# In bucketing, GpSimd adds the products with the counts in pairs of tiles, in place of VectorE

## What is computed

```python
edge_index = jnp.stack([src, dst])
h = jnp.maximum(_layernorm(x, axis=-1), 0.0)
x = x + _L0_gnn_ref(h, L0_gnn_qW, L0_gnn_kW, L0_gnn_vW, src, dst)   # attention over edges, 4 heads
h = jnp.maximum(_layernorm(x, axis=-1), 0.0)
x = x + _L1_gnn_ref(h, src, dst, L1_gnn_W, L1_gnn_b)                # softmax aggregation, linear
h = jnp.maximum(_layernorm(x, axis=-1), 0.0)
x = x + _L2_gnn_ref(h, edge_index)                                  # 10 steps of propagation
h = jnp.maximum(_layernorm(x, axis=-1), 0.0)
x = x + _L3_gnn_ref(h, edge_index, L3_gnn_W1, L3_gnn_b1, L3_gnn_W2, L3_gnn_b2)
```

## Time and profile before

| | us |
|---|---|
| device time, median of 3 runs | 3986.82 (3985.64 to 3989.67) |
| profiled execution, device time | 3985.65 |
| its span | 3983.4 |
| TensorE matmuls busy | 3849.9 (97%) |
| VectorE busy | 1767.2 (44%) |
| ScalarE busy | 1296.6 (33%) |
| GpSimd busy | 598.4 (15%) |

### The profile page before, as it was taken

How to read it: one execution, slowest core, us unless ns; L and a number is a source line. 1 busy time by engine, 2 the same in 40 slices (tenths; PEclk the granted TensorE clock), 3 DMA queues, 4 the chain that set the end, 5 groups by cost and what they waited for, 6 DMA issues and landing times.

```text
span 3983.4 us, 124087 instructions
## 1 busy us (share of the span) xinstructions
PE 3849.9 (97%) x46183; PEld 3657.0 (92%) x46183; DVE 1767.2 (44%) x4392; ACT 1296.6 (33%) x3880; POOL 598.4 (15%) x716
## 2 busy tenths in 40 slices
PE   2889999999999999999999999999999998999999
PEld 2679999999966667999999999999999998999999
DVE  8999999999982333222222222222222222331111
ACT  1248888888850111222222122122222221111110
POOL 1016666666630000000000000000000000000000
PEclk9989999999999999999999999999999999999999
DMA  1039999999973333666656665665666655667675
GB/s 41 3 74 240 232 239 231 232 236 233 232 209 111 112 109 131 204 204 204 201 205 202 201 205 200 203 205 200 204 203 201 205 201 178 203 218 213 208 216 157
DMA packets 438000, 747.71 MB, mean 188 GB/s; under 512 B 197331, under 2 KB 330579, under 8 KB 437840
## 3 DMA queue, kind: packets, MB, share of 16 engines
q1 hardware_dynamic: 433346, 744.61, 61.6%
q10 hardware_dynamic: 4494, 0.77, 0.1%
HBM read 621.82 MB, written 83.32 MB: 177 GB/s over the span
## 4 chain that ended last, share of the span: by engine, by line
PE 92%; DVE 6%; issue 1%; ACT 0%; DMA 0%; ACTq 0%; POOL 0%; DVEq 0%; SPq 0%; POOLq 0%
PE sum L1843 49%; PE sum L1477 19%; PE pk L1195 10%; PE pr L1218 7%; PE pq L1207 3%; PE pc L1231 2%; DVE onerank L814 2%; PE l L490 1%; DVE bt L786 1%; DVE prodb L803 1%; DVE vals L796 1%; PE l L474 0%; DMA X<-in_x_dram 0%; PE sum L1668 0%; DVE kv L622 0%
## 5 line engine op out<-in xcount | busy, mean ns | idle before, releaser
L1843 PE MATMUL sum<-u,ring 128*128 128x192 f16 x12005 | 993.0, 246 | 0.0
L1843 PEld LDWEIGHTS sum<-u,ring 128*128 128x128 fp8e4 x12005 | 992.0, 98 | 0.3
L1843 PE MATMUL sum<-y,ring 128*128 128x192 f16 x11662 | 962.9, 246 | 0.0
L1843 PEld LDWEIGHTS sum<-y,ring 128*128 128x128 fp8e4 x11662 | 962.2, 98 | 0.0
L1477 PE MATMUL sum<-u,ring 128*128 128x385 f16 (+1 forms) x4802 | 607.2, 288 | 6.6 <-issue 5.2
L1477 PEld LDWEIGHTS sum<-u,ring 128*128 128x128 fp8e4 x4802 | 435.1, 98 | 168.0 <-issue 8.7
L1852 DVE TENSOR_TENSOR z<-lo,sum 128x96 f32<-128x96 f32 x441 | 112.1, 254 | 986.9 <-ACT lo L1867 986.7
L1195 PE MATMUL pk<-kv,hT 128*128 128x192 f16 x4900 | 485.7, 247 | 2.0 <-DVE hT L1087 2.0
L1195 PEld LDWEIGHTS pk<-kv,hT 128*128 128x128 f16 x4900 | 409.8, 99 | 2.4 <-DVE hT L1087 2.3
L1277 ACT ACTIVATE kvs<-pk 128x384 f32<-128x384 f32 x735 | 301.0, 437 | 111.4 <-PE pk L1195 90.9
L1218 PE MATMUL pr<-wv,hs_wide 128*128 128x101 f32 x2450 | 321.3, 278 | 2.0 <-POOL wv L1148 2.0
(11 more groups left out here) (252 smaller groups left out, 3033.8 us busy)
## 6 DMA issues: line engine op xcount, KB each, us to landing
ring<-adjacency_t SPq DMA_DIRECT2D x490, 800.0 KB, 4.3
ring<-adjacency SPq DMA_DIRECT2D x147, 896.0 KB, 5.0
rows<-slot_rows_d SPq DMA_DIRECT2D x249, 320.0 KB, 4.0
adjacency<-row SPq DMA_DIRECT2D x49, 800.0 KB, 4.3
adjacency_t<-col SPq DMA_DIRECT2D x49, 800.0 KB, 4.6
col<-row SPq DMA_TRANSPOSE x245, 4.2
out_dram<-X SPq DMA_DIRECT2D x6, 336.0 KB
slot_rows_d<-T SPq DMA_DIRECT2D x2, 240.0 KB
```

What stands on the lines that cost most here:

```text
L1843: m = pe.matmul(ps[r][:, 0:2 * D], w[:, t // 2, :, t % 2], n["this"][:, t, 0:2 * D], start=t == 0, stop=t == TILES - 1)
```

## The change

The addition `prod2` leaves VectorE's queue. GpSimd gets a loop over the 25 groups: wait for the group's `prod`, wait until TensorE has read the last group's `prod2` (`ranked`), add. It signals a new semaphore `halved`, for which TensorE waits at the head of `tensor_rank` beside `prod`. `k.prod` now counts one signal per group, and all waits on it are renumbered. A semaphore that was not used (`added2`) gives way to the new one.

```diff
--- before.py
+++ after.py
@@ -782,7 +782,7 @@
             if g >= 2:
                 v.wait_ge(k.counted.sem, k.counted.at(g - 1))
                 v.wait_ge(k.val.sem, k.val.at(g - 1))
-                v.wait_ge(k.prod.sem, k.prod.at(2 * (g - 1)))
+                v.wait_ge(k.prod.sem, k.prod.at(g - 1))
             v.tensor_tensor(bt[i][:], number_2[:].unsqueeze(1).to_broadcast([P, TWOS_RUN, TILES, 2]), of_group(tile1, g),
                             ALU.is_equal).then_inc(k.bt.sem, 1)
             if g >= 2:
@@ -798,12 +798,10 @@
         def vector_before(g):
             v.wait_ge(k.before.sem, k.before.at(g + 1))
             if g:
-                v.wait_ge(k.prod.sem, k.prod.at(2 * g))
+                v.wait_ge(k.prod.sem, k.prod.at(g))
                 v.wait_ge(k.ranked.sem, k.ranked.at(g))
             v.tensor_tensor(prod[:], bt[g % 2][:], before[g % 2][:].unsqueeze(1).to_broadcast([P, TWOS_RUN, TILES, 2]),
                             ALU.mult).then_inc(k.prod.sem, 1)
-            v.wait_ge(k.prod.sem, k.prod.at(2 * g + 1))
-            v.tensor_tensor(prod2[:], prod[:, :, 0:EVEN // 2, :], prod[:, :, EVEN // 2:EVEN, :], ALU.add).then_inc(k.prod.sem, 1)
 
         def vector_place(g):
             v.wait_ge(k.rank.sem, k.rank.at(g + 1))
@@ -819,6 +817,12 @@
             pool.iota(base[:], [[GROUP, GROUPS]], base=0, channel_multiplier=0,
                       allow_small_or_imprecise_dtypes=True).then_inc(k.base1.sem, 1)
             pool.memset(tile0, 0.0).then_inc(k.base1.sem, 1)
+            for g in range(GROUPS):
+                pool.wait_ge(k.prod.sem, k.prod.at(g + 1))
+                if g:
+                    pool.wait_ge(k.ranked.sem, k.ranked.at(g))
+                pool.tensor_tensor(prod2[:], prod[:, :, 0:EVEN // 2, :], prod[:, :, EVEN // 2:EVEN, :],
+                                   ALU.add).then_inc(k.halved.sem, 1)
 
         def tensor():
             for turn in range(GROUPS + 1):
@@ -876,7 +880,8 @@
             parts += [(far[i][:, odd, j, :], pr[:, TWOS_RUN:RUN]) for odd in range(2) for j in range(half)]
             parts += [(prod[:, :, j, :], to) for j in range(EVEN, TILES)] + [(prod2[:, :, j, :], to) for j in range(EVEN // 2)]
             pe.wait_ge(k.same.sem, k.same.at(2 * g + 2))
-            pe.wait_ge(k.prod.sem, k.prod.at(2 * g + 2))
+            pe.wait_ge(k.prod.sem, k.prod.at(g + 1))
+            pe.wait_ge(k.halved.sem, k.halved.at(g + 1))
             if g:
                 pe.wait_ge(k.rank.sem, k.rank.at(g))
             for n, (part, place_of) in enumerate(parts):
@@ -905,7 +910,7 @@
                 if turn < GROUPS:
                     a.wait_ge(k.counted.sem, k.counted.at(turn + 1))
                     if turn >= 2:
-                        a.wait_ge(k.prod.sem, k.prod.at(2 * (turn - 2) + 1))
+                        a.wait_ge(k.prod.sem, k.prod.at(turn - 1))
                     a.activation(before[turn % 2][:], over(pp[turn % 2][:, 0:TILES], 2), ACT.Copy).then_inc(k.before.sem, 1)
                     projection.copy(turn)
                 if turn == EARLY:
@@ -960,7 +965,8 @@
     k.weighted, k.summed = Beat(k, "at_weighted", CP), Beat(k, "at_summed", CP)
     k.q_in, k.denom, k.inverse, k.normed = (Beat(k, f"at_{x}", 2) for x in ("q_in", "denom", "inverse", "normed"))
     k.ratio, k.totalled, k.degreed = (Beat(k, f"at_{x}", 2) for x in ("ratio", "totalled", "degreed"))
-    k.added, k.added2 = k.sig("added"), k.sig("added2")
+    k.added = k.sig("added")
+    k.halved = k.sig("halved")
     k.row_out, k.col_out = ([Beat(k, f"at_{x}{b}", n) for b in range(2)] for x, n in (("row_out", 16 * CHUNKS + 16), ("col_out", 16)))
     k.out_c = Beat(k, "at_out_c", 2 * UP)
     k.av_set = k.sig("av_set")
```

## The result

The changed kernel takes 4027.05 us (median of 4, 4025.85 to 4030.66) beside 3986.69 us for the kernel before: a ratio of 1.0100, 95% interval 1.0088 to 1.0112. The direction was forecast; the time, 4069, was not, and the range missed it by one microsecond at its low end.

The account below looks back on a forecast made before the run. VectorE was taken to bound bucketing, with delays passed on in full; 24 turns each 3.38 us longer (81.1) plus 1.4 for the last gave 82.5 us, so 4069 us, range 4028 to 4088.

Parts of the forecast that it names:

- What bounds the stage; a delay passes on in full: Bucketing: VectorE sets the pace, busy 197.52 of 200.00 us; any shift of its end shifts the rest of the kernel.
- Removal: 0.65 us a turn: VectorE in bucketing: without prod2, bt starts 0.98 us after prodb in place of 1.63.
- Length of the addition, 2.0 us: GpSimd's addition over 128x864 16-bit elements, scaled from its fp32 rows; bounds 1.66 to 2.19 us.
- the low end of 1.0 us: GpSimd's addition, should 16-bit inputs go twice as fast: about 1.0 us, giving 4045 us.
- When GpSimd may begin: behind vals: Bucketing turn: VectorE's run bt, near, far, vals keeps GpSimd out; it starts 3.78 us after prodb's start.
- rows 7 and 8: Attention trace rows: GpSimd's weighting starts 0.09 us behind VectorE's hd, read as VectorE's run keeping GpSimd out.
- B: Rival in bucketing: GpSimd gets in right behind bt, adding from 2.14 to 4.14 us; 4030 us, chance 0.10.
- B's price, 1.74 us a turn: Bucketing turn under rival B: onerank at 6.73 us after prodb's start in place of 4.99; chance 0.10.
- Rank path as what is late: Bucketing: onerank waits for rankb, 2.55 us behind the addition, with VectorE idle for nearly 4 us.
- The clock, at most 3 us: TensorE idling more at 1.2 GHz lengthens the rank path by 0.12 us a turn, at most 3 us in all.
- The range: Whole kernel: 4028 to 4088 us, holding cases A, B and E, together 0.88.
- the likeliest case: Bucketing: GpSimd adds behind vals; 4069 us, 4045 to 4074 with the addition's bounds, chance 0.74.

Follow-up runs that it names:

- a near relative: The changed kernel, with the 36 rank matmuls that need only near and far ahead of TensorE's waits for the products: 4025.31 us, ratio 1.0095.
- the run behind vals: The changed kernel, with GpSimd asking only once VectorE's vals of the next group is done: 4073.36 us, ratio 1.0212.
- three others: The changed kernel with near's and far's rank matmuls first (4025.31 us), with GpSimd's addition unused (4007.97 us), with GpSimd asking after bt (4048.43 us).

## Why the prediction was wrong, step by step

- *What bounds the stage; a delay passes on in full.* Right: 38.7 + 1.4 + 0.2 us in the stage, 40.6 at the end of attention, 40.4 between the medians.
- *Removal: 0.65 us a turn.* Right: bt 0.99 us behind prodb, and 6.94 us a turn where only this path is left.
- *Length of the addition, 2.0 us.* 1.83 undisturbed, 9% too long. The Trainium skill (GPSIMD Engine Reference, Performance versus the Vector engine) gives 4497 ns for an fp32 addition of 2048 elements; in proportion an estimate of 1.90 for 864. The measured 16-bit addition is near to it: the halved element size did not halve the time, and the low end of 1.0 us did not come true.
- *When GpSimd may begin: behind vals.* This step failed. In 23 of 24 turns GpSimd was let in behind bt, its addition ended 3.74 us after prodb's start and not 5.78, and near was held off. The step was read from rows 7 and 8, where the start behind hd came from a semaphore in the calling function, not from VectorE's run. Taken alone, those rows say nothing about which engine is let in; without them the order of asking favoured B, which the forecast had put at 0.10. The mechanism does exist, in 1 of 24 turns of the changed kernel and 12 of 24 of a near relative. Made the rule, it costs 84 us where the forecast had 82.5, with two terms off that offset each other (see the run behind vals).
- *B's price, 1.74 us a turn.* Measured 1.55, from two terms that offset in part. The addition ended 3.74 us after prodb's start, not 4.14: 0.17 of that is its shorter length, 0.23 that it was at work a little ahead of bt's end and not behind it. From there to rankb's end it took 2.71 to 2.83 us, not 2.55. The fixed part of this, 0.16 us, is the step from GpSimd to TensorE: where GpSimd asks behind vals, 0.22 us lie between its end at 162.03 and the first weight load at 162.25, while VectorE's end had needed 0.06. The rest, 0 to 0.12 us, is in the rank matmuls, slower at the lower clock.
- *Rank path as what is late.* Right: the changed kernel's VectorE waits 0.46 us for rankb, and not for the nearly 4 us of the forecast. But near, held off, is close behind it; with the rank path 0.9 us shorter it sets the turn.
- *The clock, at most 3 us.* Right, as far as the rank path goes. The stage was granted 0.77 in place of 0.92, so more time at 1.2 GHz. Single turns of the changed kernel were granted 0.68 to 0.81: at 0.81 the rank matmuls take 2.22 us from first to last, as long as in most turns of the kernel before, at 0.68 they take 2.33. Over the steady turns that is a mean of 0.05 us, some 1 us in all.
- *The range.* It held B's sum, 4030, by 2 us. It missed because B stood in it without the bounds of the addition that the likeliest case had: with a 1.66 us addition, B's sum is 4022. A rival with a chance of 0.10 belongs in a range with its own bounds.

What stays open: what decides, when VectorE's next instructions could already be issued, whether GpSimd is let in at the first boundary or after the run. By the traces both happen with the same spacing of the instructions to a hundredth of a microsecond. That the two exclude each other, and that the one that issues first blocks the other, is what the Trainium skill states (SBUF — State Buffer, Who interferes with whom). On the exclusion the traces agree: 2.59 us for the addition behind bt and 2.12 for near behind the addition, in place of 1.83 and 0.49. That the first to ask is served next, as I had read it, holds in 23 of 24 turns of the changed kernel, in 12, 12 and 14 of 24 in three others, and in all 24 where VectorE waits for bt ahead of near.

## What to carry to other kernels

In these runs an addition with two SBUF inputs, moved to GpSimd beside a VectorE that is never idle, was paid three times: by its own slower run (1.83 us beside 0.61), by its wait for VectorE's current instruction, and by the VectorE instruction that it held off. Such a move could gain only if VectorE's path had room for the last, and if nothing waited for the result; in no kernel here was that so. Before a wait in the trace is taken for a property of the chip, read every wait of that queue up to the calling function, and take the suspected one out in an experiment. And ask first whether the work is needed at all: TensorE did the same sum in 24 more matmuls for 0.54 us of its time a turn, and the turn still fell from 7.58 to 7.17 us; with near's and far's matmuls moved into TensorE's waits the kernel was 0.4% faster than before.

## What the runs showed of the hardware that I had not expected

- A GpSimd addition that asks while VectorE runs instructions with two SBUF inputs back to back was let in at the next boundary (2.59 us in all) or behind the whole run of four (4.22 us), both within one kernel. With a VectorE wait on its own preceding instruction it was the former in all 24 turns of one kernel.
- A GpSimd fill of 1.60 us disturbed none of them; an addition stretched the 0.49 us near to 2.12.
- From GpSimd's end to TensorE's first weight load 0.22 us passed, beside 0.06 us from VectorE's end.
- TensorE's rank matmuls over prodb took 36 ns each, those over prod2 in the kernel before 48 ns (24 weight loads in 1.16 us).
